# A decoder kernel: the opening stage processes 51 tiles of the context in place of 52

## The chip, the cores and the metric

The kernel runs on one core of one Trainium2 chip. The metric is the device time of one execution in microseconds, and the time of a kernel is the median over its runs.

## The reference, cut to what matters

Two decoder layers run over 1024 tokens of width 128. Each adds three things to x: a token mixer, a cross attention to a context of 6404 rows of width 96, and a mixture of experts.

```python
x = x + L0_attn(layernorm(x), ...)              # fast weights, updated chunk by chunk
x = x + L0_xattn(layernorm(x), ctx_768, ...)    # k = ctx @ Wk + bk, v = ctx @ Wv + bv, 8 heads of 16
x = x + L0_ffn(layernorm(x), ...)               # 160 experts, 8 per token
x = x + L1_attn(layernorm(x), ...)              # selective scan
x = x + L1_xattn(layernorm(x), ctx_768, mask, ...)  # 8 heads of 64, keys of unit length, one null key and value
x = x + L1_ffn(layernorm(x), ...)               # 8 experts, 2 per token
```

The context has 6404 rows, which are 50 tiles of 128 and 4 rows more. The null key of the second cross attention takes the row after the last one, so that 6405 rows matter: tiles 0 to 50. The arrays are laid out for 52 tiles (KVT = 52, KVP = 6656), so tile 51 is nothing but padding.

## The kernel before, in words

The kernel runs six stages one after another (`decoder`, line 3150). Each is a block in which all engines run programs of their own and wait for each other by semaphores; at the end of a block they meet at a barrier (line 3142), and GpSimd clears the semaphores.

The change touches the first of them, `opening_stage` (line 160). It does two independent things at once.

One is the fast-weight mixer of the first layer: layer norm, projections, three updates of the weights (each with five rounds of a matrix iteration), the output added to x chunk by chunk (`add_outputs`, line 873), then the layer norm of the new x (statistics in `norm_statistics`, lines 56 to 61, the power -0.5 on GpSimd, line 376, and `norm_apply`, line 67), its transposes (TensorE line 731, ScalarE line 543), the query projection (TensorE line 736), and the split of the queries into three bfloat16 parts (ScalarE lines 548 and 549, VectorE lines 975 to 978). This is a long chain of small steps.

The other is the context: for each tile of 128 context rows the keys and values of both cross attentions are computed, brought into the form in which the attentions need them, and stored to DRAM. The steps of tile t are spread over four ticks of a loop that each engine has in its own program (`context()`):

- tick t: TensorE projects keys (line 576) and values (line 580) of the second attention; ScalarE squares the keys (line 452) and copies the values out (line 458); VectorE sums the squares by head (line 782) and, every second tick, masks the next pair of tiles (line 754); GpSimd raises the sums to the power -0.5 (line 367).
- tick t + 1: TensorE projects keys and values of the first attention (lines 568, 569); ScalarE copies them out (lines 441, 442, 445); GpSimd splits the keys into bfloat16 parts with four instructions (lines 359 to 362); VectorE scales the keys of the second attention (line 773).
- tick t + 2: TensorE transposes the scaled keys (line 587).
- tick t + 3: ScalarE copies out their high half (line 432), VectorE their low half (line 766).

A tick has four pieces on each engine, separated by `yield`. With TICKS = KVT + 3 = 55 ticks there are 220 pieces, and `Filler` deals them out at named points of the fast-weight program. How many pieces go to each point is written down by hand in FILLS, FILLS_GRADIENT, FILLS_ROUND, FILLS_UPDATE and FILLS_END, and their sum is 220, too. The last points are these, and the pieces of ticks 51 to 54 fall on them in turn:

```python
FILLS_END = (("last0", 2), ("last1", 2), ("q_stats", 3), ("q_norm", 3), ("q_tr", 3), ("q_split", 3))
```

On VectorE the point last0 comes behind the last gated product (line 958), last1 behind the last addition to x (line 873), q_stats behind the norm statistics, q_norm behind the normalising (line 67), q_tr behind the addition of a bias to x (line 970), q_split behind the query split. A point that is reached when no piece is left does nothing.

SyncE stores pairs of tiles. For the pair n it waits until v1_done, first_mm, v0_done and k0_split have each reached 2n + 2, and for the low halves until lo_done has. The semaphores v1_done, first_mm, v0_done, k0_split and lo_done were raised by one for each tile. Behind the last pair come, in the order of SyncE's program, the rest of the split queries (lines 322, 323; they wait for q_split), the loads of the first query stacks (line 119), three patches of the stored values (lines 329 to 331; one writes zeros over tile 51 of the first attention's values) and the store of the last pair's second-attention keys (line 290).

The second stage, `xattn0_stage` (line 1002), starts with maxima over the keys (TensorE line 1265). It reads keys up to column 6448 and 51 tiles of values. `xattn1_stage` (line 2219) reads keys up to column 6416 and leaves tile 51 out, too.

Of the kernel before, what the change touches and what calls it, by code (L numbers as in the profile page):

```python
# [16 lines left out]
P = 128  # L17
# [59 lines left out]
KVT = 52  # L77
# [82 lines left out]
def opening_stage(nc, k, d):  # L160

    with ExitStack() as ctx:
# [88 lines left out]
        INVERT_AT = {at: slice(1664 * b, 1664 * b + 1664) for b, at in enumerate((0, 6, 19, 32))}  # L251
        REST = slice(INVERT_AT[0].stop, KVP)
        KV_CHUNKS = KVT // 2
        TICKS = KVT + 3
        UPDATES = CHUNKS - 1

        def need(e, semaphore, count):
# [4 lines left out]
        with nc.Block() as block:  # L262
# [77 lines left out]
            def _(e):  # L340
# [1 line left out]
                by_head = [v0_out[s][:].rearrange("p j (h f) -> p j h f", f=32) for s in range(2)]  # L342
                finished = {}

                def finish(instruction, semaphore):

                    finished[semaphore.name] = finished.get(semaphore.name, 0) + 1
                    instruction.then_inc(semaphore, 1)
                    e.wait_ge(semaphore, finished[semaphore.name])

                def context():
                    for tick in range(TICKS):
                        yield
                        yield
                        t = tick - 1
                        if 0 <= t < KVT:
                            part = lambda i: k0_parts[t // 2 % 2][:, i, P * (t % 2):P * (t % 2) + P]
                            e.wait_ge(k0_done, t + 1)
                            finish(G.tensor_tensor(kr[:], kf[:], part(0), ALU.subtract), split)
                            finish(G.tensor_tensor(part(1), kr[:], zeros[:, 0:P], ALU.add), split)  # L360
                            finish(G.tensor_tensor(kf[:], kr[:], part(1), ALU.subtract), split)
                            finish(G.tensor_tensor(part(2), kf[:], zeros[:, 0:P], ALU.add), k0_split)
                        yield
                        if tick < KVT:
                            e.wait_ge(summed, tick + 1)
# [46 lines left out]
            def _(e):  # L412
# [7 lines left out]
                def context():  # L420
                    e.wait_ge(got_real, 16)
                    invert(0)
                    e.wait_ge(load_c, 16 * LOADS_C)
                    e.wait_ge(consts, CONSTS + 2)
                    for tick in range(TICKS):
                        if tick and tick in INVERT_AT:
                            invert(tick)
                        t = tick - 3
                        if 0 <= t < KVT:
                            e.wait_ge(k1_tr, t + 1)  # L430
                            need(e, st_k1[t // 2 % 2], 16 * (t // 4))
                            ACTIVATE(k1_parts[t // 2 % 2][:, 0, :, P * (t % 2):P * (t % 2) + P], psT[:], ACT.Copy)\
                                .then_inc(hi_done, 1)
                        yield
                        t = tick - 1
                        if 0 <= t < KVT:
                            s, j = t // 2 % 2, t % 2
                            e.wait_ge(first_mm, t + 1)
                            need(e, k0_split, t)
                            need(e, st_k0[s], 16 * (t // 4))  # L440
                            ACTIVATE(kf[:], psV[:, 0:P], ACT.Identity, bias=bk0[:])
                            ACTIVATE(k0_parts[s][:, 0, P * j:P * j + P], psV[:, 0:P], ACT.Identity, bias=bk0[:])\
                                .then_inc(k0_done, 1)
                            need(e, st_v0[s], 16 * (t // 4))
                            ACTIVATE(v0_out[s][:, j, :].rearrange("p (h f) -> p h f", f=32)[:, :, 0:16],
                                     psV[:, P:2 * P].rearrange("p (h f) -> p h f", f=16), ACT.Copy).then_inc(v0_done, 1)
                        yield
                        t = tick
                        if t < KVT:
                            e.wait_ge(k1_mm, t + 1)  # L450
                            need(e, summed, t)
                            ACTIVATE(ksq[:], psK[:, t % 2, :], ACT.Square).then_inc(squared, 1)
                        yield
                        if t < KVT:
                            s, j = t // 2 % 2, t % 2
                            e.wait_ge(v1_mm, t + 1)
                            need(e, st_v1[s], 16 * (t // 4))
                            ACTIVATE(v1_out[s][:, j, :], psV[:], ACT.Copy).then_inc(v1_done, 1)
                        yield

                fill = Filler(context())
# [95 lines left out]
            def _(e):  # L557
                T = nc.tensor

                def context():  # L560
                    e.wait_ge(load_c, 16 * LOADS_C)
                    e.wait_ge(consts, CONSTS)
                    for tick in range(TICKS):
                        t = tick - 1
                        if 0 <= t < KVT:
                            e.wait_ge(v1_done, t + 1)
                            rows = ctx_in[t // 2 % 3][:, P * (t % 2):P * (t % 2) + P]
                            T.matmul(psV[:, 0:P], wk0[:], rows[0:CTX, :], start=True, stop=True)
                            T.matmul(psV[:, P:2 * P], rows, wv0[:], start=True, stop=True).then_inc(first_mm, 1)
                        yield  # L570
                        t = tick
                        if t < KVT:
                            rows = ctx_real[t // 2 % 2][:, P * (t % 2):P * (t % 2) + P]
                            e.wait_ge(masked, t // 2 + 1)
                            need(e, kn_done, t - 1)
                            T.matmul(psK[:, t % 2, :], rows, wkv1[:, 0:512], start=True, stop=True).then_inc(k1_mm, 1)
                        yield
                        if t < KVT:
# [4 lines left out]
                        if 0 <= t < KVT:  # L583
# [158 lines left out]
            def _(e):  # L742
# [3 lines left out]
                def context():  # L746
# [13 lines left out]
                    for tick in range(TICKS):  # L760
                        yield
                        t = tick - 3
                        if 0 <= t < KVT:
                            s, cols = t // 2 % 2, slice(P * (t % 2), P * (t % 2) + P)
                            e.wait_ge(hi_done, t + 1)
                            V.tensor_tensor(k1_parts[s][:, 1, :, cols], psT[:], k1_parts[s][:, 0, :, cols], ALU.subtract)\
                                .then_inc(lo_done, 1)
                        yield
                        t = tick - 1
                        if 0 <= t < KVT:  # L770
# [8 lines left out]
                        if t < KVT:  # L779
# [2493 lines left out]
```

## Time and profile before

| | |
|---|---|
| median of 3 runs | 2722.06 us (2716.48 to 2723.71) |
| the profiled execution | 2724.11 us |
| its span, first to last instruction | 2721.9 us |
| TensorE busy | 2400.1 us, 88% |
| VectorE busy | 2046.7 us, 75% |
| ScalarE busy | 1530.3 us, 56% |
| GpSimd busy | 301.8 us, 11% |
| mean granted TensorE clock | 0.925 |

In the rows, PE is TensorE's matmul, PEld its load of the stationary operand, DVE is VectorE, ACT ScalarE, POOL GpSimd and SP SyncE; a q behind the name is the engine's own sequence of waits and issues. L67 is line 67 of the kernel before. A line of the view in order of time gives the start in us from the start of the span, the duration in us, the engine, the line, the operation, what it writes <- what it reads, shapes, how many instructions are merged, and in square brackets the idle time of the engine before it with what ended it.
### The profile page before, as it was taken

The page shows a single profiled execution, that of the slowest core. Times are in us where ns is not written, and L with a number is a line of the kernel's source. Part 1 is how long each engine was busy: PE and PEld are TensorE (multiplying, and loading weights), DVE is VectorE, ACT ScalarE, POOL GpSimd, SP SyncE. Part 2 cuts the span into 40 slices and gives each one's busy share as a digit, 9 for nine tenths or more (in the row PEclk, how much of TensorE's full clock was granted, in tenths as well). Part 3 has the DMA queues.
Part 4 walks back from the last instruction along what each step waited for, and adds up shares of the span by engine and source line. Part 5 has one row for each costly group of instructions (what it writes and reads, how often), then busy time and mean ns, then how long its engine had stood idle before and what let it go on. Part 6 is the DMA issues. An engine that isn't in the chain of part 4 may idle for free. (4 is left out here: it accounts for less than half of the span.)

```text
span 2721.9 us, 34159 instructions
## 1 busy us (share of the span) xinstructions
PE 2400.1 (88%) x10276; PEld 877.3 (32%) x10276; DVE 2046.7 (75%) x3026; ACT 1530.3 (56%) x1859; POOL 301.8 (11%) x333
## 2 busy tenths in 40 slices
PE   6888677999999979999476589999999999997998
PEld 3555411222222224444123123323333332332443
DVE  5676698999995124333797889999999898976775
ACT  5555496777668843333443566667666666653111
POOL 5665500000000000000164000000000000000000
PEclk8898957999999989999688589999999999998998
DMA  5354471221100149999101431022013011111100
GB/s 139 127 169 142 131 109 35 62 66 27 28 24 27 30 114 207 212 224 192 25 0 36 97 95 37 28 63 73 28 32 105 29 29 29 31 36 61 54 0 8
DMA packets 209736, 201.51 MB, mean 74 GB/s; under 512 B 18928, under 2 KB 170005, under 8 KB 208785
## 3 DMA queue, kind: packets, MB, share of 16 engines
q1 hardware_dynamic: 209453, 199.62, 29.0%
q8 instruction: 80, 1.31, 0.2%
q14 instruction: 59, 0.48, 0.1%
q10 hardware_dynamic: 144, 0.10, 0.0%
HBM read 154.77 MB, written 41.42 MB: 72 GB/s over the span
## 5 line engine op out<-in xcount | busy, mean ns | idle before, releaser
L2795 DVE TENSOR_TENSOR y_acc<-y_acc,y_probs 128x1024 f32<-128x1024 f32 x400 | 486.9, 1217 | 35.2 <-ACT y_probs L2483 23.4
L1223 ACT ACTIVATE x_probs<-x_E 128x1024 f32<-128x1024 f32 x408 | 396.7, 1022 | 137.0 <-PE x_E L1283 135.1
L2483 ACT ACTIVATE y_probs<-y_E,y_mask_bias 128x1024 f32<-128x1024 f32 x408 | 433.1, 1111 | 71.2 <-PE y_E L2575 64.7
L1406 DVE TENSOR_REDUCE x_maxima<-x_M 128x1 f32<-128x496 f32 x660 | 411.3, 671 | 27.3 <-PE x_M L1265 17.0
L2584 PE MATMUL y_O<-y_probs,y_values 128*64 128x512 f32 x1632 | 398.5, 609 | 0.0
L2574 PE MATMUL y_E<-y_qa,y_ks 128*128 128x512 f16 x816 | 312.7, 383 | 1.5 <-ACT y_copied L2456 1.2
L2575 PE MATMUL y_E<-y_qb,y_ks 66*128 66x512 f16 x816 | 311.1, 381 | 0.0
L2456 ACT ACTIVATE y_copied<-y_M 128x1024 bf16<-128x1024 f32 (+1 forms) x164 | 162.4, 990 | 211.5 <-PE y_M L2538 211.5
L2733 DVE TENSOR_REDUCE y_maxima<-y_M 128x2 f32<-128x1024 f32 (+2 forms) x195 | 231.3, 1186 | 39.9 <-PE y_M L2538 30.3
L1867 DVE TENSOR_TENSOR f_hidden<-f_act_out,f_spread 128x512 f32<-128x512 f32 x160 | 110.7, 693 | 183.4 <-ACT f_act_out L1701 172.2
L1296 PE MATMUL x_O<-x_probs,x_values 128*32 128x512 f32 x1632 | 218.6, 608 | 0.4 <-ACT x_probs L1223 0.4
L1701 ACT ACTIVATE f_act_out<-f_b 128x512 f32<-128x512 f32 x160 | 95.4, 597 | 195.6 <-PE f_b L1760 195.6
L1283 PE MATMUL x_E<-qs,x_keys 128*128 128x512 bf16 x688 | 185.8, 384 | 6.6 <-ACT x_probs L1223 4.8
L1760 PE MATMUL f_b<-f_xnT,f_weights 128*128 128x512 f32 x320 | 170.3, 615 | 9.8 <-DMA f_weights<-f_w_in 9.8
L2538 PE MATMUL y_M<-y_ks,y_qa 64*128 64x512 f16 (+1 forms) x742 | 145.8, 390 | 27.9 <-DVE y_maxima L2733 23.0
L1765 PE MATMUL f_b<-f_hidden,f_weights 128*128 128x512 f32 x320 | 164.9, 598 | 0.0
L2584 PEld LDWEIGHTS y_O<-y_probs,y_values 128*64 128x64 f32 x1632 | 99.6, 136 | 166.4 <-issue 153.1
L2744 DVE TENSOR_TENSOR y_running<-y_running,y_copied 128x1024 bf16<-128x1024 bf16 x192 | 127.6, 665 | 8.7 <-ACT y_copied L2456 8.4
L1265 PE MATMUL x_M<-x_keys,qs 64*128 64x496 bf16 x298 | 116.9, 392 | 16.4 <-DVE x_maxima L1406 16.4
L2574 PEld LDWEIGHTS y_E<-y_qa,y_ks 128*128 128x128 f16 x816 | 80.0, 98 | 138.6 <-issue 42.3
L2992 PE MATMUL g_b<-g_w_in,g_xnT 128*128 128x512 f32 x256 | 116.9, 602 | 6.2 <-DVE g_gate L3062 3.9
L2538 PEld LDWEIGHTS y_M<-y_ks,y_qa 64*128 64x128 f16 x742 | 35.7, 93 | 262.4 <-DVE y_maxima L2733 166.2
(500 smaller groups left out, 3170.4 us busy)
## 6 DMA issues: line engine op xcount, KB each, us to landing
f_spread<-comb_dram SPq DMA_DIRECT2D x160, 256.0 KB, 6.0
y_values<-v_dram SPq DMA_DIRECT2D x208, 128.0 KB, 2.2
f_weights<-f_w_in SPq DMA_DIRECT2D x80, 256.0 KB, 6.3
v_dram<-a_v_out SPq DMA_DIRECT2D x26, 512.0 KB, 2.6
k_dram<-a_k_parts SPq DMA_DIRECT2D x26, 512.0 KB, 3.3
x_values<-v_dram SPq DMA_DIRECT2D x100, 128.0 KB, 2.2
y_ks<-k_dram SPq DMA_DIRECT2D x75, 128.0 KB, 3.0
v_dram<-a_v_out SPq DMA_DIRECT2D x26, 256.0 KB, 2.0
```

The lines of the kernel that those rows point to most:

```text
L1223: nc.scalar.activation(probs[:, n % 2, 2 * g:2 * g + 2, :], psE[:, 2 * g:2 * g + 2, :], ACT.Exp).then_inc(exped, 1)
L1283: ins = T.matmul(psE[:, j, :], key_tile(4 * (u // 2) + j, t), qs[:, u, j, :], start=True, stop=True)
L1296: ins = T.matmul(psO[32 * j:32 * j + 32, :], values[:, i, 32 * j:32 * j + 32], probs[:, n % 2, j, :], start=(t == 0), stop=(t == TILES0 - ...
L1406: V.tensor_reduce(maxima[:, 2 * h + j, qt, c:c + 1], psM[(2 * entry + j) % 3][:, 0:CHUNK0], AX.X, ALU.max).then_inc(max_done, 1)
L1760: T.matmul(gate_ps[i % ITEM_SLOTS][:], weights[:, i, 0:P], xnT[:, HALF * h:HALF * h + HALF], start=True, stop=True).then_inc(gate_mm, 1)
L2483: A(probs[:, i, :], psE[:, 2 * (i % 2):2 * (i % 2) + 2, :].rearrange("p a b -> p (a b)"), ACT.Exp, bias=mask_bias[:, bass.ds(c * TILES_IN_ ...
L2538: ins = T.matmul(out[:, j, 0:width(c)], qa[r, u, j, q0:q0 + P], ks1[r, u // 2 % 2, c * 512 + KVP * j:c * 512 + KVP * j + width(c)], start= ...
L2574: T.matmul(psE[:, 2 * slot + j, :], ks1[:, u // 2 % 2, keys], qa[:, u, j, :], start=True, stop=False)
L2575: ins = T.matmul(psE[:, 2 * slot + j, :], ks2[:, u // 2 % 2, keys], qb[:, u, j, :], start=False, stop=True)
L2584: ins = T.matmul(psO[u % 2][DH1 * j:DH1 * j + DH1, :], values[:, i, DH1 * j:DH1 * j + DH1], probs[:, i, 512 * j:512 * j + 512], start=Fals ...
L2733: V.tensor_reduce(maxima[:, u % 2, :, 2 * g, bass.ds(c, 1)], scores[:, :, 0:width(c)], AX.X, ALU.max)\
L2795: ins = V.tensor_tensor(acc[:, u % 2, :], acc[:, u % 2, :], probs[:, i, :], ALU.add)
```

## The change

The constant REAL_TILES = KVT - 1 = 51 takes the place of KVT in the opening's context loops, and TICKS becomes 54, so that there are 216 pieces. The table of points is as it was: the first 216 pieces fall where they fell, and the last points get fewer. At tile 50 five semaphores are raised by 2 in place of 1, so that SyncE's waits for the last pair come true without tile 51. KV_CHUNKS stays 26: the last pair is still stored with both its halves, the second of them with what the buffers hold. The masked context of the last pair is still computed whole. Nothing else in the program is changed.

```diff
-        TICKS = KVT + 3
+        REAL_TILES = KVT - 1
+        TICKS = REAL_TILES + 3
+
+        def ends(t):
+
+            return 2 if t == REAL_TILES - 1 else 1
...
-                def finish(instruction, semaphore):
+                def finish(instruction, semaphore, count=1):
 
-                    finished[semaphore.name] = finished.get(semaphore.name, 0) + 1
-                    instruction.then_inc(semaphore, 1)
+                    finished[semaphore.name] = finished.get(semaphore.name, 0) + count
+                    instruction.then_inc(semaphore, count)
                     e.wait_ge(semaphore, finished[semaphore.name])
...
-                        if 0 <= t < KVT:
+                        if 0 <= t < REAL_TILES:
                             part = lambda i: k0_parts[t // 2 % 2][:, i, P * (t % 2):P * (t % 2) + P]
                             e.wait_ge(k0_done, t + 1)
...
-                            finish(G.tensor_tensor(part(2), kf[:], zeros[:, 0:P], ALU.add), k0_split)
+                            finish(G.tensor_tensor(part(2), kf[:], zeros[:, 0:P], ALU.add), k0_split, ends(t))
                         yield
-                        if tick < KVT:
+                        if tick < REAL_TILES:
                             e.wait_ge(summed, tick + 1)
...
-                        if t < KVT:
+                        if t < REAL_TILES:
                             e.wait_ge(squared, t + 1)
                             need(e, rooted, t)
                             V.tensor_reduce(ksum[:], ksq[:].rearrange("p (h f) -> p h f", h=8), AX.X, ALU.add)\
```

The bounds of the other loops, on TensorE, ScalarE and VectorE, change in the same way, and `then_inc(..., 1)` becomes `then_inc(..., ends(t))` for first_mm, v0_done, v1_done and lo_done.

## Rows read from the trace of the kernel before

**Rows 1.** The page's chain of the work that ended last, share by engine

```profile
PE 5%; DVE 2%; DMA 1%; issue 0%; SPq 0%; ACT 0%; DVEq 0%
```

**Rows 2.** VectorE in order of time, 13.9 and 315 to 322; columns: start, us, what, idle before

```profile
13.91 2.13 DVE L67 TENSOR_SCALAR a_xn<-x,a_moments,a_rstd 128x128 f32<-128x128 f32 x8
...
315.38 0.42 DVE L873 TENSOR_TENSOR x<-x,a_b 128x256 f32<-128x256 f32 x1 [0.59 <-PE a_b L645]
315.83 0.69 DVE L773 SCALAR_TENSOR_TENSOR a_kn<-a_kroot,a_K 128x512 f32<-128x512 f32 x1
316.44 0.68 DVE L782 TENSOR_REDUCE a_ksum<-a_ksq 128x8 f32<-128x512 f32 x1
317.04 1.64 DVE L56 BATCH_NORM_STATS2 a_stats<-x 128x6 f32<-128x128 f32 x8
...
321.37 3.14 DVE L67 TENSOR_SCALAR a_xn<-x,a_moments,a_rstd 128x128 f32<-128x128 f32 x8 [0.57 <-POOL a_rstd L376]
```

**Rows 3.** GpSimd in order of time, 13.8 and 317 to 322

```profile
13.80 1.86 POOL L367 TENSOR_TENSOR a_kroot<-a_ksum,a_mhalf 128x8 f32<-128x8 f32 x1 [4.03 <-DVE a_ksum L782]
...
317.25 1.65 POOL L367 TENSOR_TENSOR a_kroot<-a_ksum,a_mhalf 128x8 f32<-128x8 f32 x1 [1.37 <-DVE a_ksum L782]
...
319.70 1.64 POOL L376 TENSOR_TENSOR a_rstd<-a_var,a_mhalf 128x8 f32<-128x8 f32 x1 [0.80 <-DVE a_var L61]
...
321.41 0.43 POOL L359 TENSOR_TENSOR a_kr<-a_kf,a_k_parts 128x128 f32<-128x128 f32 x1
```

**Rows 4.** Line 67 in its first use, its second, and the second's first instruction; ns min/median/max

```profile
L67 DVE TENSOR_SCALAR a_xn<-x,a_moments,a_rstd x8: 341/342/342, 13.9 to 15.7; 128x128 f32<-128x128 f32 x8
...
L67 DVE TENSOR_SCALAR a_xn<-x,a_moments,a_rstd x8: 334/444/610, 321.4 to 324.2; 128x128 f32<-128x128 f32 x8
...
L67 DVE TENSOR_SCALAR a_xn<-x,a_moments,a_rstd x1: 551/551/551, 321.4 to 321.4; 128x128 f32<-128x128 f32 x1
```

**Rows 5.** TensorE in order of time, 314 to 344

```profile
314.24 1.10 PE L645 MATMUL a_b<-a_w1t_bd,a_inner 128*128 128x64 f32 x8 [0.82 <-DVE a_inner L958]
...
315.18 1.08 PE L580 MATMUL a_V<-a_wkv,a_ctx_real 97*128 97x512 f32 x2
...
324.56 1.97 PE L731 MATMUL a_b<-ident_sb,a_xn 128*128 128x128 f32 x8 [6.91 <-DVE a_xn L67]
...
327.18 2.73 PE L736 MATMUL a_b<-a_xnT,a_wq 128*128 128x512 f32 x4
...
343.42 0.57 PE L1265 MATMUL x_E<-ks,qs 64*128 64x496 bf16 x1 [13.08 <-PEq L3142]
```

**Rows 6.** ScalarE in order of time, 325 to 330

```profile
325.71 0.60 ACT L543 ACTIVATE a_xnT<-a_b 128x512 f32<-128x512 f32 x1 [7.23 <-PE a_b L731]
...
329.09 0.69 ACT L548 ACTIVATE a_qT<-a_b,a_bq 128x512 f32<-128x512 f32 x1 [1.07 <-PE a_b L736]
```

**Rows 7.** VectorE in order of time, 328 to 335

```profile
328.66 1.22 DVE L970 TENSOR_TENSOR x<-x,a_bo 128x1024 f32<-128x1024 f32 x1
...
330.46 0.69 DVE L975 TENSOR_TENSOR a_kT<-a_qT,a_q_parts 128x512 f32<-128x512 f32 x1 [0.58 <-ACT a_q_parts L549]
...
334.62 0.43 DVE L978 CAST a_q_parts<-a_qT 128x512 bf16<-128x512 f32 x1
```

**Rows 8.** SyncE's issues in order of time, 335 to 342

```profile
335.08 0.52 SPq L322 DMA_DIRECT2D q_dram<-a_q_parts  x1
...
341.25 0.56 SPq L290 DMA_DIRECT2D k_dram<-a_k_parts  x1
```

**Rows 9.** Busy time by stretch: PE, PEld, DVE, ACT, POOL busy, clock, DMA share, GB/s

```profile
328.00:330.00 2.00, 2.00 (x7) 0.93 (x6) 1.82 (x2) 0.93 (x3) 0.00 (x0) 0.78 0.00 0
...
360.00:380.00 20.00, 14.80 (x56) 2.91 (x56) 20.00 (x35) 18.99 (x22) 0.00 (x0) 0.50 1.04 122
...
436.00:438.00 2.00, 2.00 (x8) 0.30 (x10) 0.67 (x2) 1.82 (x2) 0.00 (x0) 0.50 0.03 8
...
2250.00:2300.00 50.00, 47.60 (x214) 14.51 (x212) 43.29 (x51) 32.02 (x33) 0.00 (x0) 0.97 0.10 29
```

More of the change, by code:

```diff
@@ L428, in context @@
                         t = tick - 3
-                        if 0 <= t < KVT:
+                        if 0 <= t < REAL_TILES:
                             e.wait_ge(k1_tr, t + 1)
@@ L435, in context @@
                         t = tick - 1
-                        if 0 <= t < KVT:
+                        if 0 <= t < REAL_TILES:
                             s, j = t // 2 % 2, t % 2
@@ L445, in context @@
                             ACTIVATE(v0_out[s][:, j, :].rearrange("p (h f) -> p h f", f=32)[:, :, 0:16],
-                                     psV[:, P:2 * P].rearrange("p (h f) -> p h f", f=16), ACT.Copy).then_inc(v0_done, 1)
+                                     psV[:, P:2 * P].rearrange("p (h f) -> p h f", f=16), ACT.Copy).then_inc(v0_done, ends(t))
                         yield
                         t = tick
-                        if t < KVT:
+                        if t < REAL_TILES:
                             e.wait_ge(k1_mm, t + 1)
@@ L453, in context @@
                         yield
-                        if t < KVT:
+                        if t < REAL_TILES:
                             s, j = t // 2 % 2, t % 2
@@ L457, in context @@
                             need(e, st_v1[s], 16 * (t // 4))
-                            ACTIVATE(v1_out[s][:, j, :], psV[:], ACT.Copy).then_inc(v1_done, 1)
+                            ACTIVATE(v1_out[s][:, j, :], psV[:], ACT.Copy).then_inc(v1_done, ends(t))
                         yield
@@ L564, in context @@
                         t = tick - 1
-                        if 0 <= t < KVT:
+                        if 0 <= t < REAL_TILES:
                             e.wait_ge(v1_done, t + 1)
@@ L568, in context @@
                             T.matmul(psV[:, 0:P], wk0[:], rows[0:CTX, :], start=True, stop=True)
-                            T.matmul(psV[:, P:2 * P], rows, wv0[:], start=True, stop=True).then_inc(first_mm, 1)
+                            T.matmul(psV[:, P:2 * P], rows, wv0[:], start=True, stop=True).then_inc(first_mm, ends(t))
                         yield
                         t = tick
-                        if t < KVT:
+                        if t < REAL_TILES:
                             rows = ctx_real[t // 2 % 2][:, P * (t % 2):P * (t % 2) + P]
@@ L577, in context @@
                         yield
-                        if t < KVT:
+                        if t < REAL_TILES:
                             need(e, v0_done, t)
@@ L582, in context @@
                         t = tick - 2
-                        if 0 <= t < KVT:
+                        if 0 <= t < REAL_TILES:
                             e.wait_ge(kn_done, t + 1)
@@ L762, in context @@
                         t = tick - 3
-                        if 0 <= t < KVT:
+                        if 0 <= t < REAL_TILES:
                             s, cols = t // 2 % 2, slice(P * (t % 2), P * (t % 2) + P)
@@ L766, in context @@
                             V.tensor_tensor(k1_parts[s][:, 1, :, cols], psT[:], k1_parts[s][:, 0, :, cols], ALU.subtract)\
-                                .then_inc(lo_done, 1)
+                                .then_inc(lo_done, ends(t))
                         yield
                         t = tick - 1
-                        if 0 <= t < KVT:
+                        if 0 <= t < REAL_TILES:
                             e.wait_ge(rooted, t + 1)
@@ L778, in context @@
                         t = tick
-                        if t < KVT:
+                        if t < REAL_TILES:
                             e.wait_ge(squared, t + 1)
```

## The prediction

> **What bounds the kernel now.** I read the page's chain first. It follows only the last stage: TensorE, VectorE and one load, together some 8% of the span [rows 1]. The opening is not in it, so the question has to be put to the opening itself: the stages follow one another behind a barrier, and a microsecond that leaves the opening leaves the span only if the opening's last piece of work moves, and if the next stage is not held by something else.
>
> So I read the opening's tail engine by engine, in order of time. The fast-weight work sets its end. VectorE adds the last output to x at 315.38, runs two context pieces at 315.83 and 316.44, and only then starts the norm statistics at 317.04 [rows 2]. GpSimd gives the rstd at 319.70 for 1.64 us [rows 3], VectorE normalises x from 321.37 for 3.14 us [rows 2], TensorE waits for that with an idle gap of 6.91 us and transposes from 324.56, then projects from 327.18 [rows 5]. ScalarE reads the first projection at 329.09 [rows 6], VectorE splits it from 330.46 and ends its last split at 334.62 + 0.43 = 335.05 [rows 7]. SyncE, which waited for that, issues from 335.08 without a break until 341.25 + 0.56 = 341.81 [rows 8], and TensorE starts the next stage at 343.42 behind the barrier (PEq L3142) [rows 5]. That is the path. TensorE, ScalarE and GpSimd have slack in it.
>
> **What the change removes.** All of tile 51: on TensorE its projections (keys, values, the layer-0 pair) and four transposes; on ScalarE six copies or squares; on GpSimd one power and four splits; on VectorE three operations. No DMA is removed: the last pair of tiles is stored whole, its second half being what the buffer held before. The pieces are drawn tick by tick, so tile 51's tick 51 falls on the points last0 and last1, tick 52 on q_stats and the first piece of q_norm, and everything before tick 51 stays where it is. I go through it in the order of the path.
>
> Step 1, the reduction for tile 51 (line 782) at 316.44. It stands between the add to x and the statistics, and no idle time is noted on either side. From its start to the start of the statistics is 317.04 - 316.44 = **0.60 us** [rows 2], all on the path. What is late next is still VectorE itself: tile 50's scaling at 315.83 stays. TensorE's key projection of tile 51 goes too, but TensorE waited 0.82 us for VectorE ahead of the outputs at 314.24, so nothing is won there; the value projection, at 315.18, stood behind those outputs [rows 5].
>
> Step 2, the power for tile 51 on GpSimd at 317.25. It ends at 318.90, and GpSimd then waits 0.80 us for the variance before the rstd [rows 3]. With the variance 0.60 earlier there would still be 0.20 left. Worth nothing more; it is covered by VectorE's statistics, and if that cover were gone it would be worth up to its 1.65.
>
> Step 3, the scaling for tile 51 (line 773) on VectorE, between the statistics and the normalising. Behind it VectorE waits 0.57 us for the rstd [rows 2]. Worth nothing; with no wait there it would be worth what tile 50's takes, 0.61 from its start to the next.
>
> Step 4, the four splits on GpSimd, one every half microsecond from 321.41, each about as long as the first, 0.43 us [rows 3]. They look harmless, as nobody on the path waits for them. But the eight normalising instructions (line 67) last 3.14 us here. The same eight at 13.91 last 342 ns each, all of them; here they last from 334 to 610 ns, the first 551 [rows 4]. Beside the first four run the four splits, and the other four are short. Eight undisturbed ones take 2.13 us from start to end [rows 2]. The bound from below is that the length has another cause and stays (0); from above that all of it goes: 3.14 - 2.13 = **1.01 us**. I take the upper one, since the power at 13.80 ran beside the undisturbed eight [rows 3, 4] and four long ones against four splits is too neat to be chance.
> The Trainium skill (SBUF — State Buffer, Terms) says of VectorE and GpSimd that they share one port pair, locked for a whole instruction: "the loser **fully blocks**, it doesn't share bandwidth". By that the sum is -1.6; if the lengthening had nothing to do with it, -0.6. The trace agrees with the rule in that the waits come one for each split.
>
> Step 5, ScalarE's square, copy of values and three copies of tile 51. They fall before the transposes come back, while ScalarE idles for 7.23 us ahead of 325.71 [rows 6]. Nothing. Tile 51's high half on ScalarE and low half on VectorE come after the last read of the projections and after the last split: nothing.
>
> Step 6, the double counts. Five semaphores are raised by 2 at tile 50 in place of 1. Nobody waits more often. SyncE sees the counts of the last pair earlier, so three stores of the last pair leave earlier; the key store keeps its place behind the store of the queries. No load that anybody waits for is in flight there. Nothing.
>
> Step 7, is the gain kept to the end? TensorE's transposes of tile 50 and the two projections move as a block. The second projection could come late: if the clock stays at 0.50 until 328 to 330, where it rose before [rows 9], the two need at most 329.09 - 327.18 = 1.91 us each and the second ends at about 325.57 + 3.82 = 329.4; ScalarE's two reads of 0.7 us end before 331.1, which is when VectorE has done the first half's split (half of 335.05 - 330.46 is 2.3, from 328.85) [rows 6, 7]. Covered. SyncE's twelve issues move with it. In the next stage VectorE is busy 20.00 of 20.00 us from 360 to 380 [rows 9], so an earlier start goes straight through it.
>
> **The sum.** -0.60 - 1.01 = -1.6 us. The profiled execution took 2724.11 us (span 2721.9); so 2722.5. It stands 2.05 above the median of the three runs, 2722.06, so at the median the time is **2720.4**, 0.06% less. What a measurement of this kernel can tell from no change is about 0.3%, 8.2 us.
>
> **The rivals.**
> *Only the reduction counts.* The eight instructions stay at 3.14 us. For: bounds of step 4. Against: the pattern of rows 4. 2721.5.
> *The clock takes half of it back.* TensorE's heavy work in the next stage starts near 436 at a granted clock of 0.50, with TensorE busy 2.00 of 2.00 us [rows 9]. If the rise comes at the same moment and the work 1.6 us sooner, 1.6 us more of it run at half speed and 0.8 are lost: 2721.2. Against: nothing says that the moment is tied to the start of the kernel. The other way, if less or later of the projections runs at 0.50 in the opening, the first is up to 0.9 shorter, and VectorE's bias add (328.66 + 1.22 = 329.88 against 330.46 [rows 7]) lets 0.6 of that through: 2719.8.
> *Slower, by clock dips.* The second cross attention keeps TensorE busy, and yet its granted clock averages 0.97 from 2250 to 2300 [rows 9]: one dip costs 50 x 0.03 = 1.5 us. Nothing there is touched, but its work stands 1.6 us elsewhere. One dip more leaves 2721.9; from the second on the kernel is slower: 2723.4. For: the three runs of the one kernel already differ by 7.2 us. Against: as many dips may go as come.
> *Slower, by code.* The straight code of the opening gets shorter, so every loop behind it lies elsewhere. No row of TensorE or ScalarE shows time lost to issue ahead of its work in those loops, so I price it as one dip, at 1.5 us, and not slower on its own. The Trainium skill (Runtime: NRT & Kernel Launch, Instruction fetch mechanics) says that code comes in blocks and a taken branch out of the two at hand stalls for a fetch; by it the time could move either way, and no run here shows it yet.
> *The change doesn't reach the end.* SyncE's issues, 335.08 to 341.81, would have to be held by something other than the split. It is not noted. 2722.1.
>
> **How the numbers follow.** Chances: the forecast 0.45; only the reduction 0.13; half taken back 0.12; the faster side of the clock 0.10; dips 0.10; code 0.05; nothing arrives 0.05. All of them lie within 3 us of the time before, far inside 0.3%; what is beyond it can only come from a term I have not seen, of either sign, on which I put 0.10, taken out of all the cases: 0.06 faster, 0.04 slower. So 0.90 for within. The range is made of the runs more than of the cases: they lay between 2716.48 and 2723.71. The lowest less 2.2 (1.6 and the clock's 0.6) is 2714.3, the highest with two dips, 2723.71 - 1.6 + 3.0, is 2725.1; rounded outwards, 2714.0 to 2726.0.
>
> **What would show it.** Step 1: the statistics start 0.6 us after the start of tile 50's scaling, in place of 317.04 - 315.83 = 1.21. Step 4: line 67 in its second use at about 342 ns for all eight, 2.13 in all, and no GpSimd work after the rstd. Step 7: the distance from the add to x to the next stage's first matmul, 343.42 - 315.38 = 28.04 before, is 26.4. Wrong would be: line 67 still long; that distance above 27.4; or a stage after the opening that differs by more than 2 us, which would mean that the time is decided by what I called dips. In that case the total says nothing of the change.

## The result, and the profile after

In 20 runs each the changed kernel took 2715.51 us (2703.94 to 2720.48), the kernel before 2720.66 us (2715.49 to 2735.56): a ratio of **0.9975**, interval 0.9964 to 0.9986. That is 6.8 us less (interval 3.8 to 9.8), where 1.6 was forecast. The time lies in the forecast's range and the change is below 0.3%, but the interval leaves out 1.6, so the sum lacked something. That the time lies in the range is no proof of the sum: the range was made of the spread of the runs more than of its terms. One run of all that follow, 354.18 us of `open_splits`, fell into the chip's slower state and is left out.

The profiled execution of the changed kernel took 2713.56 us:

```profile
span 2711.6 us, 34114 instructions
...
PE 2388.7 (88%) x10264; PEld 872.7 (32%) x10264; DVE 2044.0 (75%) x3023; ACT 1528.7 (56%) x1853; POOL 299.1 (11%) x328
```

The path of the opening once more. VectorE in order of time (start, us, what, idle before), to hold against [rows 2, 7]:

```profile
315.17 0.42 DVE L879 TENSOR_TENSOR x<-x,a_b 128x256 f32<-128x256 f32 x1 [0.59 <-PE a_b L651]
315.62 0.69 DVE L779 SCALAR_TENSOR_TENSOR a_kn<-a_kroot,a_K 128x512 f32<-128x512 f32 x1
...
320.58 2.14 DVE L67 TENSOR_SCALAR a_xn<-x,a_moments,a_rstd 128x128 f32<-128x128 f32 x8 [1.17 <-POOL a_rstd L382]
...
332.87 0.43 DVE L984 CAST a_q_parts<-a_qT 128x512 bf16<-128x512 f32 x1
```

Line 67's second use, ns min/median/max [rows 4], and GpSimd from 316 to 342 [rows 3]:

```profile
L67 DVE TENSOR_SCALAR a_xn<-x,a_moments,a_rstd x8: 339/341/345, 320.6 to 322.4; 128x128 f32<-128x128 f32 x8
```

```profile
318.89 1.65 POOL L382 TENSOR_TENSOR a_rstd<-a_var,a_mhalf 128x8 f32<-128x8 f32 x1 [3.15 <-DVE a_var L61]
341.33 0.29 POOL L1178 MEMSET x_maxima<- 128x224 f32 x1 [20.79 <-POOLq L3148]
```

TensorE [rows 5], ScalarE's read of the second projection [rows 6] and SyncE's issues [rows 8]:

```profile
322.77 1.97 PE L737 MATMUL a_b<-ident_sb,a_xn 128*128 128x128 f32 x8 [6.79 <-DVE a_xn L67]
...
325.39 3.52 PE L742 MATMUL a_b<-a_xnT,a_wq 128*128 128x512 f32 x4
...
341.55 0.57 PE L1271 MATMUL x_E<-ks,qs 64*128 64x496 bf16 x1 [12.65 <-PEq L3148]
```

```profile
328.94 0.69 ACT L554 ACTIVATE a_qT<-a_b,a_bq 128x512 f32<-128x512 f32 x1 [0.34 <-PE a_b L742]
```

```profile
333.32 0.52 SPq L328 DMA_DIRECT2D q_dram<-a_q_parts  x1
...
339.35 0.56 SPq L296 DMA_DIRECT2D k_dram<-a_k_parts  x1
```

The reader sees the forecast path, shorter at two places: the reduction is gone from behind line 779, and line 67 takes 2.14 us in place of 3.14, with nothing on GpSimd beside it. From the add to x to the next stage's first matmul it is 341.55 - 315.17 = **26.38 us**, against 28.04 before and 26.4 forecast. The second projection did run longer at the low clock (line 742: 3.52, before 2.73), and it was hidden, as ScalarE read it before VectorE wanted it.

So the opening gave 1.66 us. Where is the rest? The stages' lengths, in us, from the barrier instructions (L3142 before, L3148 after):

| us | opening | first attention | experts | scan | second attention | experts |
|---|---|---|---|---|---|---|
| before | 343.0 | 645.2 | 305.9 | 188.2 | 1025.9 | 209.8 |
| after | 341.0 | 643.3 | 302.0 | 185.4 | 1026.6 | 209.4 |

The two first profiles differ by 10.3 us, more than the two kernels do. The stages of experts and scan, alike in both programs, differ by 3.9 and 2.8; the experiments show that they scatter as much for one kernel. The 1.9 in the first attention is another matter: counted from the stage's first matmul, its instructions stand within about 0.1 us of each other in both programs for the first 87 us, and then the changed kernel gets ahead at two places. This is the first place, VectorE around 440, before and after:

```profile
437.33 1.26 DVE L1406 TENSOR_REDUCE x_maxima<-x_M 128x1 f32<-128x496 f32 x2 [3.30 <-PE x_M L1265]
439.05 6.45 DVE L1406 TENSOR_REDUCE x_maxima<-x_M 128x1 f32<-128x496 f32 x10 [0.46 <-PE x_M L1265]
```

```profile
435.10 7.76 DVE L1412 TENSOR_REDUCE x_maxima<-x_M 128x1 f32<-128x496 f32 x12 [2.95 <-PE x_M L1271]
```

VectorE waits for TensorE there, and TensorE's granted clock is just rising from 0.50 to 1.00 (columns as in [rows 9]), before and after:

```profile
438.00:439.00 1.00, 1.00 (x11) 0.15 (x4) 0.58 (x2) 0.00 (x0) 0.00 (x0) 0.95 0.00 0
```

```profile
434.00:435.00 1.00, 1.00 (x5) 0.10 (x3) 0.00 (x0) 0.98 (x2) 0.00 (x0) 0.76 0.00 0
```

A mean of 0.95 is 0.1 us at half clock and 0.9 at full, so the rise was at 438.1; 0.76 puts it at 434.5. Counted from the stage's first matmul that is 94.7 us before and 92.9 after: the rise comes earlier in the changed kernel's stage, and VectorE's waits are shorter by 3.30 + 0.46 - 2.95 = 0.8 us.

The second place is some 105 us into the stage. TensorE there (its rows with an idle gap from 438 to 457, and to 452 after), before and after:

```profile
448.39 0.59 PE L1265 MATMUL x_M<-ks,qs 64*128 64x496 bf16 x1 [1.91 <-DVE x_maxima L1406]
...
456.02 0.38 PE L1265 MATMUL x_M<-ks,qs 64*128 64x496 bf16 x1 [0.88 <-DVE x_maxima L1406]
```

```profile
445.76 0.38 PE L1271 MATMUL x_M<-ks,qs 64*128 64x496 bf16 x1 [1.91 <-DVE x_maxima L1412]
...
451.90 0.38 PE L1271 MATMUL x_M<-ks,qs 64*128 64x496 bf16 x1 [0.87 <-DVE x_maxima L1412]
```

The stretches around that gap, first before, then after:

```profile
446.00:448.00 2.00, 0.49 (x8) 0.00 (x0) 1.97 (x2) 0.72 (x1) 0.00 (x0) 1.00 0.11 33
448.00:450.00 2.00, 1.61 (x5) 0.53 (x6) 1.90 (x4) 0.01 (x1) 0.00 (x0) 0.59 0.55 139
450.00:452.00 2.00, 2.00 (x12) 0.31 (x10) 0.91 (x3) 1.93 (x2) 0.00 (x0) 0.56 0.00 0
```

```profile
444.00:446.00 2.00, 0.24 (x2) 0.10 (x2) 1.97 (x3) 0.09 (x1) 0.00 (x0) 1.00 0.44 107
446.00:448.00 2.00, 2.00 (x16) 0.56 (x14) 1.99 (x4) 1.28 (x2) 0.00 (x0) 1.00 0.23 65
```

TensorE waits 1.91 us for the same maxima in both. Before, the granted clock falls to half behind the wait (0.59, 0.56), and VectorE, which otherwise sets the pace there, is busy only 0.91 of the 2 us from 450; after, the clock stays at 1.00. The end of this gap is 448.39 - 343.42 = 104.97 us into the stage before and 445.76 - 341.55 = 104.21 after: **0.8 us** had come with the earlier rise. From there to the next such gap it is 456.02 - 448.39 = 7.63 us with the fall and 451.90 - 445.76 = 6.14 without: the fall costs **1.5 us**. Together they are 2.25 us, and neither was in my sum. At the stage's end 1.9 of them are left.

### The profile page after: what moved, and what is told of

Read it like the earlier page. It is cut to its first block and busy times, and to the rows that moved or that the text cites. A ratio compares the mean times of both kernels' runs of the same rounds, so it can differ in the third digit from the quotient of the medians.

```text
span 2711.6 us, 34114 instructions
## 1 busy us (share of the span) xinstructions
PE 2388.7 (88%) x10264; PEld 872.7 (32%) x10264; DVE 2044.0 (75%) x3023; ACT 1528.7 (56%) x1853; POOL 299.1 (11%) x328
```

## The experiments

Beside each variant the kernel before was run on the same chip; ratios are against those runs. "The distance" is the time from the add to x to the next stage's first matmul, "the fall" that of the clock some 105 us into the first attention. Line numbers of variants lie a few lines off.

**1. How well two whole kernels can be told apart.** `control` is the kernel before, `after2` and `after3` the changed one, without edits.

> The kernel before, unchanged, run as if it were a change: what a comparison of two equal kernels gives. All theories: ratio 1.000, and how far from it says what the others can tell. Its trace also says how much the stages behind the opening differ between two executions of one program (before: barriers at 343.0, 988.2, 1294.1, 1482.3, 2508.2, 2718.0).

> The changed kernel again, unchanged. Theory 'chance' (the true gain is the opening's 1.7 us, the first comparison drew low): ratio about 0.9994, stages behind the opening no shorter on average than before. Theories 'place in time' and 'code': ratio 0.9975 again, 5 to 7 us. What one comparison can tell apart is some 2.8 us either way, so only the two together decide.

> The changed kernel a third time, beside before on this chip. 'Chance': 1.7 us below before. 'Place in time': 1.7 + 2.0 = 3.7 below, no fall of the clock 105 us into the next stage. 'Code': 5 to 7 below.

Measured: control 2718.20 us, 1.0000 (0.9986 to 1.0013); after2 2716.38, 0.9988 (0.9966 to 1.0010); after3 2712.42, 0.9974 (0.9962 to 0.9985). The three comparisons of the changed kernel, weighted by their intervals, make 6.5 us, give or take 2.0. In the traces of these and of the whole variants below the first experts' stage takes from 296.1 (delay17) to 303.9 us (delay08), whatever the kernel (control 301.1; the first profile of before 305.9), and the scan 184.9 to 190.8. So a stage table of two single traces settles nothing there. The fall is in control's trace, not in those of after2 and after3.

**2. Does the shift of the code matter?** `pad` gives the changed kernel back as many instructions on each engine as the kernel before has (TensorE 8 matmuls and transposes and 4 waits, ScalarE 6, VectorE 3, GpSimd 5), behind the path:

```diff
+                for i in range(4):
+                    T.matmul(psV[:, 8 * i:8 * i + 8], wq0[:], xnT[:, 0:8], start=True, stop=True)
+                for i in range(4):
+                    T.transpose(psK[:, 0, P * i:P * i + P], kn[:, 0, 0:P], ident[:])
...
+                    ACTIVATE(spare[:, i:i + 1], half[:, 0:1], ACT.Copy)
...
+                V.tensor_scalar(gsum[:, 0:1], gn[:, 0:1], 0.25, None, ALU.mult)
...
+                for _ in range(5):
+                    finish(G.tensor_tensor(kroot[:], ksum[:], mhalf[:, 0:8], ALU.add), split)
```

> The changed kernel with as many tiny instructions put back behind the opening's path as tile 51 took away, engine by engine, so that the code of all later stages lies where it lay before. Opening as in the changed kernel (distance from the add to x to the next stage's first matmul 26.4). Theory 'place in time' (the later stages stand earlier against moments of the clock that are tied to the start): as the changed kernel, some 5 to 7 us below before. Theory 'code': only the opening's 1.7 us stay, ratio 0.9994. Theory 'chance': 0.9994 too, and the changed kernel again as well.

Measured: 2716.86 us, 0.9990 (0.9976 to 1.0004), distance 25.96, no fall. The interval holds both no gain and most of the gain, so the total doesn't decide. The trace says more: the fall is gone with the code length of before. What remained open of the gain isn't shown to be code, nor excluded.

**3. Where did line 67's extra microsecond come from?** The opening alone, five stages left out: `open_before`, `open_after`, and `open_splits`, the latter being open_after with four GpSimd instructions put back behind the rstd:

```diff
                 power(rstd[:], var[:], mhalf[:, 0:8])
+                for _ in range(2):
+                    finish(G.tensor_tensor(kr[:], kf[:], zeros[:, 0:P], ALU.subtract), split)
+                    finish(G.tensor_tensor(kf[:], kr[:], zeros[:, 0:P], ALU.add), split)
```

> The kernel before with the opening alone: all five stages behind it left out, a wait for the opening's last loads in their place, x stored. The base for the next two; about 345 us. Its runs should lie closer together than those of the whole kernel, as the long stages are gone.

> The changed kernel with the opening alone. If the steps of the prediction are the whole of what the change does in the opening: 1.6 to 1.7 us below the opening before. If the opening gains more than the one trace shows (by the clock or the stores): more, up to 5.

> The changed kernel with the opening alone, and four GpSimd instructions over 128x128 put back behind the rstd, where tile 51's splits ran beside the normalising; nobody waits for them. If line 67 was long because of them: line 67 back at some 3.1 us in place of 2.13, and the time 1.0 us above the opening after. If it was long for another reason: line 67 at 2.13, same time.

Measured: 351.06, 348.67 and 350.29 us (5 runs each; ranges overlap: 348.43 to 352.38, 348.09 to 349.41, 347.71 to 350.86). The totals lean the expected way, the rows decide. Line 67 in open_after and in open_splits, and the latter's GpSimd:

```profile
L67 DVE TENSOR_SCALAR a_xn<-x,a_moments,a_rstd x8: 337/341/347, 320.2 to 322.0; 128x128 f32<-128x128 f32 x8
```

```profile
L67 DVE TENSOR_SCALAR a_xn<-x,a_moments,a_rstd x8: 333/456/610, 320.5 to 323.3; 128x128 f32<-128x128 f32 x8
```

```profile
320.53 0.45 POOL L414 TENSOR_TENSOR a_kr<-a_kf,a_zeros 128x128 f32<-128x128 f32 x1
...
322.12 0.45 POOL L415 TENSOR_TENSOR a_kf<-a_kr,a_zeros 128x128 f32<-128x128 f32 x1
```

Four GpSimd instructions of 0.45 us alone bring back 610 ns and a total of 3.20 us (2.14 in the whole changed kernel without them, 3.14 in open_before). Step 4 is shown.

**4. Is it the earlier start that counts, and in proportion?** A reduction that nobody reads is put ahead of the norm statistics, on the path: in `delay17` of 1536 elements, in `delay34` of 3216, in `delay08` of 720, each in the changed kernel; in `bdelay17` 1536 in the kernel before.

```diff
                 fill("last1")
+                V.tensor_reduce(gsum[:, 0:1], sq[:].rearrange("p t a b -> p (t a b)")[:, 0:1536], AX.X, ALU.max)
                 norm_statistics(nc, step, x, stats, moments, 1e-5, var[:]).then_inc(to_pow, 1)
```

> The changed kernel with one reduction over 1536 elements on VectorE ahead of the norm statistics, about 1.7 us on the opening's path, so that the later stages start when they started before, with the changed kernel's code. Theory 'place in time': as before, ratio 1.000, later stages as long as before. Theory 'code': 1.7 us over the changed kernel, so 3.5 to 5.5 below before. Theory 'chance': 1.000.

> The same with a reduction over 3216 elements, about 3.4 us, one instruction as well. Theory 'place in time': not in proportion to the delay; if the moments come every so many microseconds, another 1.7 us can bring the short later stages back, 1.7 us over before less 5. Theories 'code' and 'chance': 1.7 us over the one with half the delay.

> The changed kernel with a reduction over 720 elements, about 0.8 us, half of what takes the changed kernel back to before. Theory 'place in time': the fall is there or not according to the start alone; no theory says which for this start, it shows how wide the place is. Theory 'chance': 0.8 us over the changed kernel, whichever that is.

> The kernel before, tile 51 and all, with the reduction over 1536 elements (1.66 us) ahead of the norm statistics: the opposite shift to the change's. Theory 'place in time' (the next stage's short fall of the clock, some 105 us after its first matmul, which stands in the traces of before, control and delay17 and in none of after, after2, pad and delay34, hangs on where the stage starts against the clock's own moments): the fall is gone here as well, VectorE from the stage's first copy to its 150th instruction 1.9 to 2.2 us shorter, and the whole not slower than before by more than 0.5 us, though it does 1.7 us more. Theories 'code' and 'chance': the fall comes as often as not, and 1.7 us over before, ratio 1.0006.

The delay lands where it should (VectorE in delay17):

```profile
313.96 0.69 DVE L779 SCALAR_TENSOR_TENSOR a_kn<-a_kroot,a_K 128x512 f32<-128x512 f32 x1
314.57 1.75 DVE L969 TENSOR_REDUCE a_gsum<-a_sq 128x1 f32<-128x1536 f32 x1
```

| | added on the path | distance | us | ratio | clock falls in the first attention |
|---|---|---|---|---|---|
| delay08 | 0.9 | 27.27 | 2715.03 | 0.9981 (0.9966 to 0.9997) | no |
| delay17 | 1.66 | 27.94 | 2723.32 | 1.0010 (0.9993 to 1.0026) | yes |
| delay34 | 3.4 | 29.37 | 2717.14 | 0.9994 (0.9979 to 1.0009) | no |
| bdelay17 | 1.66, to before | 29.02 | 2718.61 | 0.9988 (0.9976 to 1.0001) | no |

Of the 1.66 us put into the kernel before, only 29.02 - 28.04 = 0.98 reached the next stage. In bdelay17 the second projection (line 736, here 737) ran wholly at full clock, 2.05 us in place of 2.73, and VectorE's wait of 0.58 us ahead of the split was gone. If only the length of the opening counted, delay34 would be the slowest and bdelay17 would stand 1.0 above before. Neither is so: more delay went with less time. The intervals are wide, and delay17's single runs reach from 2708.56 to 2728.92, its profiled one being the lowest, so the totals only lean that way. The traces are plain. bdelay17 is the kernel before with more work, and behind the same gap (TensorE 448.99, 1.91 idle) the clock holds where before it fell; in delay17 (gap's end 446.48) it falls:

```profile
449.00:451.00 2.00, 2.00 (x12) 0.65 (x16) 1.98 (x4) 1.05 (x2) 0.00 (x0) 1.00 0.27 83
```

```profile
446.00:448.00 2.00, 1.52 (x5) 0.54 (x6) 1.90 (x4) 0.00 (x0) 0.00 (x0) 0.63 0.63 150
```

**5. The gain without the noisy stages.** `two_before` and `two_after` are the opening and the first attention; `three_before` and `three_after` have the experts' stage too.

```diff
-            k.run(moe0_stage, d)
-        for stage in (mamba_stage, xattn1_stage, moe1_stage):
-            k.run(stage, d)
```

> The kernel before cut off behind the first cross attention: opening and first attention alone, the other four stages left out. The base for the next one; about 995 us, with the fall of the clock 105 us into the attention. Its runs should lie closer together than those of the whole kernel.

> The changed kernel cut off at the same place. Prediction on record (opening alone): 1.6 us below. 'Place in time' (the clock's fall in the attention is gone): 1.7 + 2.0 = 3.7 us below, with VectorE's stretch from the attention's first copy to its 150th instruction some 2 us shorter.

> The kernel before cut off behind the first mixture of experts: three stages, the other three left out. About 1300 us; its runs further apart again, since the experts' stage was between 296 and 306 us long in the traces so far.

> The changed kernel cut off at the same place. If all that the change gives is there at the end of the attention: 3.7 us below as well. If the rest of the whole kernel's 5 to 7 us arises in the experts' stage: 5 to 7 below.

Measured: two_before 992.11 us (991.40 to 993.69), two_after 988.30 (987.15 to 989.14), 5 runs each, ranges apart: **3.8 us**. TensorE's gap ends at 445.88 in the one and at 443.32 in the other; the stretches behind it:

```profile
446.00:448.00 2.00, 2.00 (x6) 0.44 (x4) 1.66 (x3) 0.52 (x1) 0.00 (x0) 0.50 0.26 67
448.00:450.00 2.00, 2.00 (x11) 0.30 (x10) 1.14 (x2) 1.42 (x2) 0.00 (x0) 0.67 0.00 0
```

```profile
444.00:446.00 2.00, 2.00 (x16) 0.44 (x13) 1.98 (x4) 1.72 (x2) 0.00 (x0) 1.00 0.01 0
```

The fall is in the one and not in the other, and the distances are 27.85 and 26.34 us. But the 3.8 isn't the sum of one pair of traces: the two profiled executions differ by 989.6 - 987.3 = 2.3 us. Of what two_after has won by 110 us into the stage, some 1.8 us is lost further on, most of it where its clock is at half from 926.5 to 933.3 us, 6.8 us long, against 3.4 at the same place in two_before. So 3.8 rests on the medians of 5 runs each, and the traces show of which parts it can be made.

With the experts' stage the gain drowns, against both expectations: three_before 1291.83 us (1291.55 to 1296.29), three_after 1297.99 (1288.40 to 1303.24). TensorE's waits in these two traces name one source, the loads of expert weights:

```profile
PE f_b L1760 <- DMA f_weights<-f_w_in: 6.8, 3, 4.5
```

```profile
PE f_b L1766 <- DMA f_weights<-f_w_in: 15.8, 16, 4.5
```

In the whole kernels' traces these waits are 6.4 (delay34) to 11.0 us (the first profile of after; before 9.8), so they don't follow the change.

**6. A store less.** The change leaves the zero store over tile 51's rows of v0 in SyncE's last issues; `nopatch` takes it out of the changed kernel. `two_nopatch` and `two_bdelay` are nopatch and bdelay17, cut as in experiment 5.

```diff
-                sp.dma_start(d.v0_dram[:, KVT - 1, :], zeros[:]).then_inc(patched, 16)
...
-                sp.wait_ge(k.patched, 48)
+                sp.wait_ge(k.patched, 32)
```

> The changed kernel without the one store that writes zeros over tile 51 of the first attention's values, which nothing reads; SyncE issues eleven DMAs instead of twelve in the opening's tail. All theories: the distance from the add to x to the next stage's first matmul 26.4 less 0.38 = 26.0. By 'place in time' the fall stays away and the whole is 0.4 below the changed kernel.

> The kernel before with the reduction of 1.66 us ahead of the norm statistics, cut off behind the first cross attention. 'Place in time': no fall of the clock 105 us into the attention, so 1.66 - 1.9 = 0.2 us below what the cut kernel before takes, near 992. Without it: 1.7 above, near 993.8. Compared with the cut kernel of this call (changed, without the patch, by 'place in time' 1.7 + 1.9 + 0.4 = 4.0 below the cut kernel before): 3.8 above it, or 5.7 if the added work costs what it takes.

> The changed kernel without the store of zeros over tile 51 of the first attention's values, cut off at the same place: 0.4 us below the cut changed kernel (988.3), so near 987.9.

Measured: nopatch 2714.75 us, 0.9985 (0.9972 to 0.9997), beside after3's 2712.42 on the same chip; the distance falls from 26.38 to 25.44, and the total shows nothing of it. Only some 0.4 of these 0.94 us is the store: the rest is VectorE's wait of 0.55 us ahead of the split, gone because the clock rose earlier. In three_after, where the store is left in, that wait is gone too and the distance is 25.89. two_nopatch 988.61 us (986.92 to 989.33), two_bdelay 991.47 (990.34 to 996.89). Cut, the kernel before with 1.66 us of work more took 0.6 us less than without it (on another chip, with a spread as large: no more than a sign). The two differ by 2.9 us, where the distances (28.97 and 25.42) would ask for 3.6; neither trace has the fall.

**All traces together.** From the clock's last fall before the first attention to that stage's first matmul. In before, in after and in open_before that fall is seen here:

```profile
335.00:336.00 1.00, 0.00 (x0) 0.00 (x0) 0.65 (x2) 0.00 (x0) 0.00 (x0) 0.85 0.85 217
336.00:337.00 1.00, 0.00 (x0) 0.00 (x0) 0.00 (x0) 0.00 (x0) 0.00 (x0) 0.50 0.72 141
```

```profile
331.00:332.00 1.00, 0.00 (x0) 0.00 (x0) 0.96 (x3) 0.00 (x0) 0.00 (x0) 1.00 0.00 0
332.00:333.00 1.00, 0.00 (x0) 0.00 (x0) 0.93 (x3) 0.00 (x0) 0.00 (x0) 0.54 0.72 141
```

```profile
335.00:336.00 1.00, 0.00 (x0) 0.00 (x0) 0.76 (x2) 0.00 (x0) 0.00 (x0) 0.80 0.91 219
```

A clock of 0.85 is 0.7 us at full and 0.3 at half, so before it is 343.42 - 335.7 = 7.7; after, 341.55 - 332.1 = 9.5.

| from the fall to the first matmul, us | kernels | fall in the attention |
|---|---|---|
| 7.6 to 7.7 | before, control, two_before, three_before | 4 of 4 |
| 8.0 to 8.6 | two_nopatch, nopatch, bdelay17, two_bdelay, pad, delay34 | 0 of 6 |
| 8.7 to 10.3 | three_after, after2, after, after3, delay08, two_after | 0 of 6 |
| 11.0 | delay17 | 1 of 1 |

The clock then stays at half until its rise, and from the fall to that rise it is 102.4 us in 16 of the 17 traces (before 438.1 - 335.7, after 434.5 - 332.1; delay17: 105.8). So whoever starts later behind the fall has the rise earlier in the stage: the end of the gap of 1.91 us lies 105.0 to 105.1 us into the stage in the first and the last line of the table, 104.8 with the shortest distance of the spared (two_nopatch) and 103.9 with the longest (two_after). The absence of the second fall gives another 1.5 us in each of the 12.

The kernel before begins that stage at the same distance from the clock's own fall, within 0.2 us, in four executions on at least two chips, and each time the clock falls again 105 us on. Whoever starts 8.0 to 10.3 us behind is spared. How closely a program keeps its distance isn't settled, though: the five traces of the changed kernel lie from 8.7 to 10.3. And in a fifth trace of the opening before, open_before, the fall came 335.6 - 315.71 = 19.9 us after the add to x, against 20.3 in before (335.7 - 315.38) and the other three. It has no attention stage; had it one, it would by a distance of 27.9 us have started some 8.0 behind the fall, like two_nopatch, which was spared. That is an estimate from these rows.

## Why the prediction was right and wrong

**Steps 1 to 3, right.** The statistics start 0.61 us after the start of tile 50's scaling (315.62 to 316.23), before 1.21. VectorE's wait for the rstd grew from 0.57 to 1.17, as the scaling of tile 51 left from behind the statistics: nothing won, nothing lost.

**Step 4, right.** 1.00 of the 1.01 us. It was the step with the widest bounds, and taking the upper one for the pattern (four long ones, four splits, and a power that disturbed nobody) held; open_splits makes it cause and not coincidence. Each GpSimd instruction of 0.45 us cost VectorE (3.20 - 2.14) / 4 = 0.27 us. The Trainium skill (SBUF — State Buffer, Terms) names a mechanism, a pair of ports held by one of the two engines for a whole instruction. The rows of the splits agree with it. The power at 13.80 doesn't: it lasted 1.86 us beside eight undisturbed instructions of 341 to 342 ns [rows 3, 4]. So the cause, the four splits, is shown, and how they delay VectorE is not.

**Steps 5 and 6, right.** ScalarE still idles 7.30 us ahead of its first copy of the transposes (line 549, before 543), and SyncE's issues run from 333.32 to 339.91, 6.59 us against 6.73.

**Step 7, wrong.** "An earlier start goes straight through it." I had shown that the next stage is bound by VectorE over 20 us and took that for the whole of it. At 437.33 and 439.05 VectorE waits for TensorE instead, 3.76 us in all, and there the granted clock decides. What failed is a term of the sum that wasn't there: the stage's length depends on where its start stands against the clock. It is 2.25 us by 110 us into the stage (0.8 by the earlier rise, 1.5 by the fall that is gone) and 1.9 at its end, more than either term that I had.

**The rival that was nearest had the right place and the wrong sign.** It let the clock take back 0.8 us, "if the rise comes at the same moment". The rise didn't: it came 102.4 us after the opening's last fall in both, that fall came 3.6 us earlier (335.7, 332.1), and the work only 1.87 (343.42, 341.55). So 0.8 was given, and not taken. The same rival had a faster side, a second projection that runs at full clock and lets up to 0.6 us through; bdelay17, nopatch and three_after show that one, in the opening, but not the two first profiles. The rival by dips had priced one at 1.5 us, which is what this fall cost, but had placed it in the second attention and held that as many come as go.

I dismissed all this because "nothing says that the moment is tied to the start of the kernel". The last table says that it is loosely tied by the end of the opening: the before kind lay within 0.2 us in four traces and 0.4 off in a fifth, the changed kernel within 1.6 us in five. Four traces with the fall and five without are good evidence that the shift doesn't average out over runs as I took for granted, and no proof that it comes every time. Why the opening comes into step isn't shown. I would argue that work at half clock until a rise evens out differences of phase, and no run tests that. Two things in the profile of before could have told me: VectorE's waits for TensorE around the rise at 438.1, and a 1.91 us idle of TensorE followed by a clock of 0.59. I had read 436 to 438 and 2250 to 2300 [rows 9], and not what came 10 us after the first.

**Code, as priced, not seen.** The rival by the Trainium skill (Runtime: NRT & Kernel Launch, Instruction fetch mechanics) let the time move either way. Apart from the two places at the clock, the attention stage's instructions stand within about 0.1 us of each other in the two first profiles for some 590 us, and pad's fall is gone though its code is as long as before. No run here shows a fetch that cost time; the later stages' scatter would hide one of a microsecond.

**The size.** Shown are 1.66 us in the opening and 1.9 to 2.25 us in the attention, together 3.6 to 3.9, and 3.8 by the medians of the cut kernels. The whole kernels differ by 6.5, give or take 2.0. What lies between, 0.7 to 4.7 us, **stays open**: a further effect of the phase in the experts' or the scan stage is possible, and so is a good part of chance, as the first comparison (6.8) and after3 (7.1) are high and after2 (3.3) isn't. The scatter of the experts' stage, 296.1 to 305.9 us over the traces of whole kernels, doesn't let 12 runs decide it.

## What to carry to other kernels

A saving ahead of a stage isn't just passed on by it. Look in the stages behind for a rise of TensorE's granted clock with another engine waiting, and for short TensorE idle gaps followed by a lower clock: what is saved or added ahead of them can cost or save more than itself, so judge a change of a microsecond or two also with small delays put on the path. If long stages scatter, cut the program behind the stage of interest: 5 runs each of the cut kernels stood apart by 3.8 us, where 12 of the whole one (after2) could not be told from no change. And where GpSimd works beside VectorE's fp32 scaling, read VectorE's single durations: the price stands on an engine that the removed work isn't on.

## What was not expected of the hardware

- The clock's last fall in the opening comes nearly in step with the program: 7.6 to 7.7 us ahead of the next stage's first matmul in four executions of the before kind. The Trainium skill (TensorE: Matmul & The Clock Gate, What's actually happening) calls the chip's watch on activity free-running; that the same gap of 1.91 us is punished in 5 traces and not in 12, by its moment, agrees with it. That four executions of one program come out so close I hadn't taken from it, and the 8.7 to 10.3 us of the changed kernel show how much room is left.
- In 16 of 17 traces the clock, once fallen there, rose again after 102.4 us, although TensorE had worked at half clock since the stage's first matmul.
- 1.66 us of added work on the path took the fall out of the kernel before (bdelay17) and put it into the changed one (delay17).
